# GpSimd sums four blocks of exponentials for one ones product, and row buffers are used in place

## Chip, cores and metric

One core of one Trainium2 chip runs the whole program. The metric is the device time in microseconds of one execution (median of three runs). TensorE (PE), VectorE (DVE), ScalarE (ACT), GpSimd (POOL) and SyncE (SP, which only issues DMAs here) each work through a fixed list of instructions in order; semaphores connect them.

## What is computed

A transformer block on x of shape 4 x 1024 x 512: layer norm, attention with 16 heads of 32, a projection, layer norm and a residual, then a gated feed-forward part (512 to 2048 to 512, weights stored as integers), again with norm and residual. The part that the change touches:

```python
scores = jnp.einsum('bsnh,btnh->bnst', k, q) / math.sqrt(HEAD_SIZE)
ones = jnp.ones_like(scores)
scores = jnp.triu(scores) + -10000.0 * jnp.tril(ones, k=-1)
attn = jax.nn.softmax(scores, axis=2)
out = jnp.einsum('bnkq,bnkh->bqnh', attn, v)
out = out.reshape(b, s, NUM_HEADS * HEAD_SIZE)
return out @ Wo + bo
```

The softmax runs over the first of the two sequence axes, and a column q sees the rows up to q.

## The kernel before

**Groups and steps.** Attention is done in 16 groups n (4 batches b, 4 groups of 4 heads, g = n mod 4). A group has 10 steps (STEPS): steps 0 to 2 take the first 512 queries (j = 0), steps 3 to 9 the second 512 (j = 1, kb = 0 to 6). A step takes one block kb of 128 keys (the last step of each j takes two short ones). The blocks kb = 0 to 3 of j = 1, steps 3 to 6, are wholly unmasked.

**One step on each engine.** TensorE makes the scores of four heads (score, L747); ScalarE writes their exponentials to Pt (L881), which has two buffers, so that step s + 2 overwrites those of step s. For the diagonal blocks (kb >= 4j) GpSimd then zeroes the masked part (L1180, two heads to an instruction). A step later TensorE multiplies the exponentials by a block of ones into PSUM bank DEN ("den", the softmax sums) and by V into bank NUM ("num"), both at L767, 8 matrix instructions of 512 columns each. Into the same loop are woven the maxima of the next group's scores ("mjob": PE L723 and L731, DVE L1006), the projections "qk", "vproj" and "woproj" (12 matmuls each at L710), at most one a step, and the layer-norm work of rows.

**Order.** order_of_jobs() writes one list PLAN; every engine walks it and takes its share, so each queue has the order of the list. A step emits: mjob, den and num of the step before, the four scores, invert and normalise where a j has ended, turns, the other row jobs, and at its end the projection that projections() names. row_work() assigns row jobs to steps by costs. Where a job is a "qk", GpSimd has a subtraction (L1173); a "dev" job is three small GpSimd instructions (L1134, L1137, L1145) that follow statistics of VectorE and precede a ScalarE normalisation (L811).

**Rows.** For each 128 rows t after woproj: yt (L1048), statistics, dev, wo_z into x1 (ACT), residual x1 + xr (DVE L1059), statistics, dev, norm2 (ACT), turn2 (PE transposes, ACT and DVE write x2s, DMA to x2d). yt, xr, x1 and x2s have two buffers each, by t mod 2. SP issues, in the list's order, among others 24 DMAs per group for "packs", the load of xr for t + 2 and the store of x1 at "residual", and the store of x2s at "turn2".

**PSUM.** Scores and maxima share five banks in turn, so that an mjob's second to fourth head wait until ScalarE has read the scores of the first to third head.

After attention the feed-forward part runs (gate_up at L781, down at L798), with the last row jobs in its first slots.

## Time and profile before

| | |
|---|---|
| median of three runs | 1789.68 us (1789.48 to 1794.05) |
| the profiled execution | 1788.66 us |
| its span | 1786.9 us |
| PE busy | 1636.9 us (92%) |
| DVE busy | 952.0 us (53%) |
| ACT busy | 744.8 us (42%) |
| POOL busy | 372.0 us (21%) |
| mean granted TensorE clock | 0.97 |

Attention runs from about 129 to 1090 us of the span, the feed-forward part from there to the end. Group 3 is the stretch 308.1 to 363.5 us, group 4 363.5 to 427.8, group 6 493.5 to 556.2, group 7 556.2 to 611.6, group 8 611.6 to 677.6, group 14 984.5 to 1039.2, group 15 1039.2 to 1090.5. Busy times are sums over instructions, with overlaps on one engine counted once; matmul ends are modelled, so that a run of them lasts about 0.2 us less than the row's figure suggests when the next one follows. A row of the timeline merges neighbouring instructions of one kind.

### The profile page before, as it was taken

The numbers are of one execution on the slowest core, as the hardware profiler recorded it, in microseconds if no ns is written. First come the engines' busy times: TensorE is split into PE (matmuls) and PEld (weight loads), VectorE is DVE, ScalarE is ACT, GpSimd is POOL, SyncE is SP. The second block draws the span as 40 slices with busy tenths as digits, with TensorE's granted clock in tenths as the row PEclk, the third lists the DMA queues.
The fourth block names the chain that finished last, engine by engine and source line by source line (L and its number), as shares of the span: only waits on it lengthen the run. The fifth ranks groups of instructions, "written<-read, shape, count | busy, mean of one in ns | idle before, by whom it ended". The sixth has DMA issues, their size and how long they took to land.

```text
span 1786.9 us, 25458 instructions
## 1 busy us (share of the span) xinstructions
PE 1636.9 (92%) x10015; PEld 691.6 (39%) x10016; DVE 952.0 (53%) x1785; ACT 744.8 (42%) x1207; POOL 372.0 (21%) x718
## 2 busy tenths in 40 slices
PE   2579999999989989999999879999999999999997
PEld 1223433333334433333333224444444444444443
DVE  3575656566666566755676623355334343435254
ACT  4314645556555556555465444323222222222221
POOL 2201422234233234222332232011000000000000
PEclk9889999999999999999999989999999999999999
DMA  6100121123122112201231453112010111110000
GB/s 220 45 21 16 48 61 33 28 77 102 31 71 55 49 56 82 71 22 47 54 93 43 136 186 136 42 56 92 30 41 36 36 36 36 42 53 28 21 24 24
DMA packets 59463, 106.28 MB, mean 59 GB/s; under 512 B 11472, under 2 KB 11472, under 8 KB 59088
## 3 DMA queue, kind: packets, MB, share of 16 engines
q1 hardware_dynamic: 59344, 104.66, 19.1%
q8 instruction: 79, 1.29, 0.3%
q14 instruction: 40, 0.33, 0.1%
HBM read 54.02 MB, written 25.17 MB: 44 GB/s over the span
## 4 chain that ended last, share of the span: by engine, by line
PE 75%; DVE 10%; ACT 9%; POOL 3%; issue 2%; DMA 1%; ACTq 0%; DVEq 0%; POOLq 0%
PE ps L781 24%; PE ps L710 17%; PE ps L767 13%; PE ps L798 12%; ACT pt L881 6%; PE ps L747 5%; DVE mcol L1006 4%; PE ps L723 2%; PE ps L731 2%; PE ps L677 1%; DVE st L908 1%; POOL rs L1137 1%; DMA xin<-in_x 1%; DVE v L996 1%; POOL rs L1145 0%
## 5 line engine op out<-in xcount | busy, mean ns | idle before, releaser
L881 ACT ACTIVATE pt<-ps,nrm 128x512 f32<-128x512 f32 (+1 forms) x640 | 360.7, 645 | 318.4 <-PE ps L747 317.9
L781 PE MATMUL ps<-x2in,gu 128*128 128x512 f16 x2048 | 464.3, 380 | 1.5 <-DVE yt L1048 1.5
L1006 DVE TENSOR_REDUCE mcol<-ps 128x1 f32<-128x512 f32 (+3 forms) x768 | 370.4, 548 | 117.3 <-PE ps L731 76.6
L781 PEld LDWEIGHTS ps<-x2in,gu 128*128 128x128 f16 x2048 | 200.7, 98 | 242.8 <-issue 2.4
L1081 DVE SCALAR_TENSOR_TENSOR hf<-ps,usc,sg 128x512 f32<-128x512 f32 x128 | 96.1, 751 | 265.3 <-PE ps L781 261.3
L798 PE MATMUL ps<-wd,hh 128*128 128x512 f16 x512 | 194.0, 379 | 0.0
L798 PE MATMUL ps<-wd,hl 128*128 128x512 f16 x512 | 194.0, 379 | 0.0
L897 ACT ACTIVATE hh<-hf 128x512 f16<-128x512 f32 x128 | 80.7, 630 | 256.5 <-DVE hf L1081 242.9
L767 PE MATMUL ps<-pt,ones 128*32 128x512 f32 (+3 forms) x1536 | 170.0, 508 | 18.1 <-POOL pt L1180 17.4
L747 PE MATMUL ps<-qpack,kpack 98*128 98x512 f16 (+3 forms) x768 | 165.4, 335 | 19.6 <-DVE mcol L1006 18.1
L1180 POOL TENSOR_SCALAR_AFFINE_SELECT pt<-pt 128x256 f32<-128x256 f32 (+1 forms) x192 | 95.7, 498 | 418.9 <-ACT pt L881 417.7
L892 ACT ACTIVATE sg<-ps,gsc 128x512 f32<-128x512 f32 x128 | 87.7, 685 | 220.7 <-PE ps L781 220.6
L1134 POOL TENSOR_SCALAR rs<-mv 128x1 f32<-128x1 f32 x128 | 24.6, 192 | 688.8 <-DVE mv L912 682.5
L767 PE MATMUL ps<-pt,v 128*32 128x512 f32 (+3 forms) x1536 | 165.9, 504 | 0.0
L1084 DVE TENSOR_TENSOR hl<-hf,hh 128x512 f16<-128x512 f32 x128 | 88.6, 692 | 96.6 <-ACT hh L897 96.6
L723 PE MATMUL ps<-stage 32*128 32x512 f16 (+3 forms) x768 | 102.1, 334 | 31.9 <-ACT pt L881 18.3
L747 PEld LDWEIGHTS ps<-qpack,kpack 98*128 98x128 f16 x768 | 59.4, 99 | 177.1 <-issue 113.5
L1173 POOL TENSOR_TENSOR stage<-tq,stage 128x512 f16<-128x512 f32 x64 | 74.4, 1163 | 158.4 <-ACT tq L871 158.4
L767 PEld LDWEIGHTS ps<-pt,v 128*32 128x32 f32 x1536 | 54.1, 112 | 75.5 <-issue 64.8
L677 PE MATMUL ps<-ident,xn 128*128 128x128 f32 x256 | 45.1, 305 | 36.1 <-ACT xn L811 27.4
L710 PE MATMUL ps<-xTh,wh 128*128 128x512 f16 x256 | 71.9, 406 | 6.7 <-ACT tq L871 6.7
L723 PEld LDWEIGHTS ps<-stage 32*128 32x128 f16 x768 | 27.3, 91 | 126.6 <-issue 51.2
(109 smaller groups left out, 1585.7 us busy)
## 6 DMA issues: line engine op xcount, KB each, us to landing
qpack<-stage SPq DMA_DIRECT2D x192, 64.0 KB, 2.0
kpack<-stage SPq DMA_DIRECT2D x192, 64.0 KB, 2.0
xin<-in_x SPq DMA_DIRECT2D x32, 256.0 KB, 2.7
xr<-in_x SPq DMA_DIRECT2D x32, 256.0 KB, 3.1
x1d<-x SPq DMA_DIRECT2D x32, 256.0 KB, 3.3
x2d<-x2s SPq DMA_DIRECT2D x32, 256.0 KB, 2.0
x2in<-x2d SPq DMA_DIRECT2D x8, 1024.0 KB, 5.6
x1in<-x1d SPq DMA_DIRECT2D x8, 1024.0 KB, 5.4
```

The source lines that it names most:

```text
L710: mm = pe.matmul(bk, lhsT, rhs, start=i == 0, stop=i == 11)
L723: mm = pe.matmul(bk[:, at:at + w], stage[rows, 0, 0, qb * 128:(qb + 1) * 128], stage[rows, 1, 0, k0:k0 + w], start=part == 0 or not diag, ...
L747: mm = pe.matmul(bk[:, at:at + 512 - q0], kp[0:98, h, kb_ * 128:(kb_ + 1) * 128], qp[0:98, h, j * 512 + q0:(j + 1) * 512], start=True, sto ...
L767: mm = pe.matmul((DEN if kind == "den" else NUM)[rows, q0:512], heads, Pt[:, ks, h, at:at + 512 - q0], start=kb_ == 0, stop=kb_ == 4 * j + 3)
L781: mm = pe.matmul(bk, GU[:, c, m, i * 128:(i + 1) * 128], x2in[:, 1 - k, :, p, c, :], start=p == 0 and c == 0, stop=p == 1 and c == 3)
L798: mm = pe.matmul(ps[:, 4 + s, :], src[:, n % 4, s * 128:(s + 1) * 128], WD[:, i, :], start=i == 0 and p == 0, stop=i == 15 and p == 1)
L881: act.activation(Pt[:, (step - 1) % 2, h, off:512], ps[:, BANK[job], off:512], ACT.Exp, scale=esc).then_inc(s_ex, 1)
L892: act.activation(sg[:, n % 2, :], ps[:, BANK["gate", n], :], ACT.Silu, scale=gsc[:, i:i + 1]).then_inc(s_sg, 1)
L1006: mm = dve.tensor_reduce(mcol[:, n % 2, col:col + 1], ps[:, BANK["max", n, i, h], at:at + w], AX.X, ALU.max)
L1081: dve.scalar_tensor_tensor(out=hf[:, n % 2, :], in0=ps[:, BANK["up", n], :], scalar=usc[:, i:i + 1], in1=sg[:, n % 2, :], op0=ALU.mult, op ...
L1084: dve.tensor_tensor(hl[:, n % 4, :], hf[:, n % 2, :], hh[:, n % 4, :], ALU.subtract).then_inc(s_hl, 1)
L1180: pool.affine_select(out=of, in_=of, compare_op=ALU.is_ge, fill=0.0, base=0, pattern=[[0, 2], [0, len(blocks(j, kb))], [1, 128]], channel_ ...
```

## The change

For the blocks kb = 0 to 3 of the second queries the ones products are left out. The exponentials of kb = 0 go to a third buffer of Pt (number 2); GpSimd adds those of kb = 1, 2 and 3 to it in place, one instruction for two heads (128 x 1024 float32), so two instructions for each of three blocks ("sum"). One ones product of the result, "den" n, 1, 0, is emitted in step 9. The exponentials that reuse a buffer now wait for the sum that reads it too (L881's wait). The sum of step s's block is emitted in step s + 1, after num.

In the list, dev jobs now stand at the head of their step, before mjob. For b > 0 and g = 0 the "qk" projections stand in steps 0, 2, 3, 7 in place of 1, 3, 7, 9 and woproj in 1, 5, 8, 9 in place of 0, 2, 5, 8. For room, the quotient is written into rec (atf goes), z into yt and the residual into xr (x1 goes), and x2s has one buffer; grow moves over Pt. The load of xr for t + 2 moves from residual t to turn2 t and waits for the store of xr t to land; turn2 waits for the store of x2s t - 1; woproj's yt waits for residual t - 2. In the feed-forward part the last woproj jobs stand in every second slot.

```diff
-        for i, s in enumerate(((1, 3, 7, 9), (0, 1, 2, 3), (1, 3, 7, 9), (1, 3, 5, 8))[g]):
+        for i, s in enumerate(((0, 2, 3, 7) if b else (1, 3, 7, 9), (0, 1, 2, 3), (1, 3, 7, 9), (1, 3, 5, 8))[g]):
             out[s] = ("qk", n + 2, i % 2, i // 2)
...
-        for i, s in enumerate(((0, 2, 5, 8), (5, 8))[g]):
+        for i, s in enumerate(((1, 5, 8, 9), (5, 8))[g]):
...
-            if kind == "wo_z" and ("wo_z", t - 2) in at and at.get(("norm2", t - 2), step) >= step:
+            if kind == "residual" and ("wo_stats", t - 2) in at and at.get(("turn2", t - 2), step) >= step:
...
+            here = rows.get(NS * n + s, [])
+            plan += [("dev", DEV_FOR[job[0]], job[1]) for job in here if job[0] in DEV_FOR]
             lot, of = (s + EARLY, n + 1) if s < NS - EARLY else (s + EARLY - NS, n + 2)
             if of < NG:
                 add(("mjob", of, lot))
             if pend is not None:
-                plan += [("den",) + pend, ("num",) + pend]
+                summed = pend[1] == 1 and pend[2] < 4
+                if not summed:
+                    add(("den",) + pend)
+                add(("num",) + pend)
+                if summed and pend[2] > 0:
+                    add(("sum",) + pend)
+                if s == NS - 1:
+                    add(("den", n, 1, 0))
             plan += [("score", n, j, kb, h) for h in range(4)]
             if pend is not None and last(*pend[1:]):
                 plan += [("invert",) + pend[:2], ("normalise",) + pend[:2]]
             if s == NS - EARLY and n + 1 < NG:
                 plan += [("mjoin", n + 1), ("mturn", n + 1)]
-            here = rows.get(NS * n + s, [])
             plan += [job for job in here if job[0] in ("ln1_turn", "turn2")]
-            for job in here:
-                if job[0] not in ("ln1_turn", "turn2"):
-                    plan += with_dev(job)
+            plan += [job for job in here if job[0] not in ("ln1_turn", "turn2")]
...
+    left = list(range(started, NT))
+    for i in range(2 * len(left) + len(LN2) - 1):
+        tail.append([each for k, t in enumerate(left) if 0 <= i - 2 * k <= len(LN2)
+                     for each in with_dev(((("woproj",) + LN2)[i - 2 * k], t))])
...
+SUMMED = [i for i, (j, kb) in enumerate(STEPS) if j == 1 and kb < 4]
+PBUF, BEFORE, used_by = {}, {}, {}
+for step in range(1, NS * NG + 1):
+    n, i = divmod(step - 1, NS)
+    buf = 2 if i == SUMMED[0] else (n * (NS - 1) + i - (i > SUMMED[0])) % 2
+    PBUF[step], BEFORE[step] = buf, used_by.get(buf)
+    used_by[buf] = step
+
...
-        Pt = A("pt", [128, 2, 4, 512], F32)
+        Pt = A("pt", [128, 3, 4, 512], F32)
+        grow = Map(A.at - 16384)("grow", [128, 2, 2048], F32)
...
+            def load_xr(t):
+                if t >= 2:
+                    e.wait_ge(d_o1[t % 2], 16 * (t // 2))
+                    e.wait_ge(s_xn, NORMED["turn2", t - 2])
+                sp.dma_start(xr[:, t % 2, :], xf[t * 128:(t + 1) * 128, :]).then_inc(d_xr[t % 2], 16)
+
...
-                        if t % 8 < 6:
-                            e.wait_ge(s_x1, NO[job])
-                            sp.dma_start(xr[:, t % 2, :], xf[(t + 2) * 128:(t + 3) * 128, :]).then_inc(d_xr[t % 2], 16)
                         e.wait_ge(s_x1, NO[job])
-                        sp.dma_start(x1d[t * 128:(t + 1) * 128, :], x1[:, t % 2, :]).then_inc(d_o1[t % 2], 16)
+                        sp.dma_start(x1d[t * 128:(t + 1) * 128, :], xr[:, t % 2, :]).then_inc(d_o1[t % 2], 16)
                     else:
-                        e.wait_ge(s_us, 2)
-                        if t >= 2:
-                            e.wait_ge(s_x1, NO["residual", t - 2])
-                        sp.dma_start(xr[:, t % 2, :], xf[t * 128:(t + 1) * 128, :]).then_inc(d_xr[t % 2], 16)
+                        load_xr(t)
                 elif kind == "turn2":
                     t = a[0]
+                    if t % 8 < 6:
+                        load_xr(t + 2)
                     e.wait_ge(s_x2h, NO[job])
                     e.wait_ge(s_x2l, NO[job])
-                    sp.dma_start(x2d[t], x2s[:, t % 2, :, :, :].rearrange("p a c n -> p (a c n)")
-                                 ).then_inc(d_o2[t % 2], 16)
+                    sp.dma_start(x2d[t], x2s[:].rearrange("p a c n -> p (a c n)")).then_inc(d_o2[t % 2], 16)
...
-                    ks = (STEP[a] - 1) % 2
+                    ks = PBUF[STEP[a]]
                     if kind == "den":
                         e.wait_ge(s_const, 7)
-                    if kb == 0 and (n, j) != (0, 0):
-                        e.wait_ge(s_dt if kind == "den" else s_at, 2 * n + j)
+                        if kb == 4 * j and (n, j) != (0, 0):
+                            e.wait_ge(s_dt, 2 * n + j)
+                        if kb < 4 * j:
+                            e.wait_ge(s_sum, 2 * NO["sum", n, 1, 3])
+                    elif kb == 0 and (n, j) != (0, 0):
+                        e.wait_ge(s_at, 2 * n + j)
...
-                                           Pt[:, ks, h, at:at + 512 - q0], start=kb_ == 0, stop=kb_ == 4 * j + 3)
+                                           Pt[:, ks, h, at:at + 512 - q0],
+                                           start=kb_ == (4 * j if kind == "den" else 0),
+                                           stop=kb_ == 4 * j + 3)
...
-                    if t >= 2:
-                        e.wait_ge(d_o2[t % 2], 16 * (t // 2))
-                    act.activation(x2s[:, t % 2, 0, :, :], ps[:, BANK[job], :].rearrange("p (c n) -> p c n", c=4),
+                    if t >= 1:
+                        e.wait_ge(d_o2[(t - 1) % 2], 16 * ((t - 1) // 2 + 1))
+                    act.activation(x2s[:, 0, :, :], ps[:, BANK[job], :].rearrange("p (c n) -> p c n", c=4),
...
-                    if step > 2:
-                        e.wait_ge(s_num, step - 2)
+                    if BEFORE[step] is not None:
+                        before = divmod(BEFORE[step] - 1, NS)
+                        e.wait_ge(s_num, BEFORE[step])
+                        if before[1] == SUMMED[0]:
+                            e.wait_ge(s_den, NO["den", before[0], 1, 0])
+                        elif before[1] in SUMMED:
+                            e.wait_ge(s_sum, 2 * NO[("sum", before[0]) + STEPS[before[1]]])
+                    if step > 1:
+                        e.wait_ge(s_us, 2)
                     e.wait_ge(s_sc, NO[job])
-                    act.activation(Pt[:, (step - 1) % 2, h, off:512], ps[:, BANK[job], off:512], ACT.Exp, scale=esc
+                    act.activation(Pt[:, PBUF[step], h, off:512], ps[:, BANK[job], off:512], ACT.Exp, scale=esc
...
-                    e.wait_ge(s_den, STEP[n, j, 4 * j + 2])
+                    e.wait_ge(s_den, NO["den", n, j, 4 * j + 2])
+                    if NO[job] > 1:
+                        e.wait_ge(s_al, NO[job] - 1)
...
-                        e.wait_ge(s_z, NO["wo_z", t - 2])
+                        e.wait_ge(s_x1, NO["residual", t - 2])
...
-                    dve.tensor_tensor(x1[:, k, :], x1[:, k, :], xr[:, k, :], ALU.add).then_inc(s_x1, 1)
+                    dve.tensor_tensor(xr[:, k, :], yt[:, k, :], xr[:, k, :], ALU.add).then_inc(s_x1, 1)
...
+                elif kind == "sum":
+                    n, j, kb = a
+                    e.wait_ge(s_num, STEP[n, 1, 0])
+                    for h in (0, 2):
+                        e.wait_ge(s_ex, NO["score", n, j, kb, h + 1])
+                        if kb > 1:
+                            e.wait_ge(s_sum, 2 * NO[job] - 3 + h // 2)
+                        pool.tensor_tensor(Pt[:, 2, h:h + 2, :], Pt[:, 2, h:h + 2, :], Pt[:, PBUF[STEP[a]], h:h + 2, :],
+                                           ALU.add).then_inc(s_sum, 1)
```

## Rows read from the trace of the kernel before

**Rows 1.** The page: busy shares, and the granted clock in 40 slices.
```profile
PE 1636.9 (92%) x10015; PEld 691.6 (39%) x10016; DVE 952.0 (53%) x1785; ACT 744.8 (42%) x1207; POOL 372.0 (21%) x718
PEclk9889999999999999999999989999999999999999
```

**Rows 2.** Stretch, its length, busy us of PE, PEld, DVE, ACT, POOL; PEclk; DMA.
```profile
308.10:363.50 55.40, 54.51 (x419) 21.72 (x417) 32.23 (x67) 29.09 (x50) 15.26 (x24) 1.00 0.15 39
363.50:427.80 64.30, 59.20 (x435) 24.07 (x434) 46.04 (x95) 37.07 (x62) 22.35 (x46) 0.97 0.27 79
...
493.50:556.20 62.70, 57.85 (x439) 23.55 (x439) 39.83 (x81) 34.21 (x58) 18.86 (x35) 1.00 0.21 60
...
984.50:1039.20 54.70, 42.35 (x299) 14.35 (x297) 29.03 (x56) 24.95 (x46) 15.66 (x26) 0.91 0.47 141
1039.20:1090.50 51.30, 41.89 (x276) 14.24 (x275) 14.81 (x24) 23.18 (x41) 19.45 (x27) 0.93 0.54 178
1090.50:1786.90 696.40, 681.87 (x3164) 310.29 (x3164) 293.00 (x467) 184.13 (x280) 42.82 (x111) 0.99 0.12 43
```

**Rows 3.** Timeline, group 7, steps 4 to 8: start, duration, instruction, idle before.
```profile
579.00 2.42 ACT L881 ACTIVATE pt<-ps,nrm 128x512 f32<-128x512 f32 x4 [1.11 <-PE ps L747]
...
587.20 1.06 PE L767 MATMUL ps<-pt,ones 128*32 128x512 f32 x8
...
588.08 1.04 PE L767 MATMUL ps<-pt,v 128*32 128x512 f32 x8
...
588.50 1.16 POOL L1173 TENSOR_TENSOR stage<-tq,stage 128x512 f16<-128x512 f32 x1 [9.01 <-ACT tq L871]
...
589.54 2.42 ACT L881 ACTIVATE pt<-ps,nrm 128x512 f32<-128x512 f32 x4 [1.12 <-PE ps L747]
...
594.43 2.42 ACT L881 ACTIVATE pt<-ps,nrm 128x512 f32<-128x512 f32 x4 [2.47 <-PE ps L747]
...
598.11 1.06 PE L767 MATMUL ps<-pt,ones 128*32 128x512 f32 x8
```

**Rows 4.** GpSimd's groups of instructions: busy, mean ns, idle before.
```profile
L1137 POOL TENSOR_TENSOR rs<-rs,half 128x1 f32<-128x1 f32 x128 | 72.1, 563 | 10.7 <-POOL rs L1134 0.2
L1180 POOL TENSOR_SCALAR_AFFINE_SELECT pt<-pt 128x256 f32<-128x256 f32 x128 | 54.5, 426 | 345.4 <-ACT pt L881 344.4 <-DVE atf L1039 0.7
...
L1192 POOL TENSOR_TENSOR atl<-atf,ath 128x512 f16<-128x512 f32 x32 | 37.1, 1161 | 2.7
L1145 POOL TENSOR_SCALAR rs<-rs,mv 128x1 f32<-128x1 f32 x96 | 27.9, 291 | 9.9
L1134 POOL TENSOR_SCALAR rs<-mv 128x1 f32<-128x1 f32 x128 | 24.6, 192 | 688.8 <-DVE mv L912 682.5
```

**Rows 5.** Timeline, group 6: exponentials of steps 4, 5; residual, dev; den of step 8.
```profile
522.65 1.26 ACT L881 ACTIVATE pt<-ps,nrm 128x512 f32<-128x512 f32 x2
...
527.78 2.42 ACT L881 ACTIVATE pt<-ps,nrm 128x512 f32<-128x512 f32 x4 [2.23 <-PE ps L747]
...
528.58 0.68 DVE L1059 TENSOR_TENSOR x<-x,xr 128x512 f32<-128x512 f32 x1
...
530.30 0.19 POOL L1134 TENSOR_SCALAR rs<-mv 128x1 f32<-128x1 f32 x1 [6.31 <-DVE mv L912]
...
542.71 1.06 PE L767 MATMUL ps<-pt,ones 128*32 128x512 f32 x8
```

**Rows 6.** Timeline around 892 us: two tensor-tensor operations on two engines.
```profile
891.89 1.15 POOL L1173 TENSOR_TENSOR stage<-tq,stage 128x512 f16<-128x512 f32 x1 [2.34 <-ACT tq L871]
...
892.21 1.38 DVE L1059 TENSOR_TENSOR x<-x,xr 128x512 f32<-128x512 f32 x1
```

**Rows 7.** Timeline of VectorE in group 8, step 3.
```profile
629.40 0.75 DVE L1048 SCALAR_TENSOR_TENSOR yt<-ps,nrm,bo_b 128x512 f32<-128x512 f32 x1 [6.09 <-ACT x L811]
```

**Rows 8.** TensorE's waits, 130 to 1090 us: total, times, longest.
```profile
PE ps L767 <- POOL pt L1180: 17.4, 11, 2.5
```

More of the change, by code:

```diff
@@ L220, in order_of_jobs @@
     started = max(job[1] for job in plan if job[0] == "woproj") + 1
-    for lot in staged(("woproj",) + LN2, list(range(started, NT))):
-        tail.append([each for job in lot for each in with_dev(job)])
+    left = list(range(started, NT))
+    for i in range(2 * len(left) + len(LN2) - 1):
+        tail.append([each for k, t in enumerate(left) if 0 <= i - 2 * k <= len(LN2)
+                     for each in with_dev(((("woproj",) + LN2)[i - 2 * k], t))])
     plan += [("load_x2", 1), ("load_x1", 0), ("load_x1", 1), ("load_ds",)]
@@ L387, in build @@
         atT = [A(f"at{p}", [128, 5, S], F16) for p in "hl"]
-        atf = A("atf", [128, 512], F32)
         rec = A("rec", [128, 512], F32)
@@ L393, in build @@
         xn = A("xn", [128, 2, 512], F32)
-        rows_at = A.at
         xr = A("xr", [128, 2, 512], F32)
         yt = A("yt", [128, 2, 512], F32)
-        x1 = A("x1", [128, 2, 512], F32)
-        x2s = A("x2s", [128, 2, 2, 4, 128], F16)
-        grow = Map(rows_at)("grow", [128, 2, 2048], F32)
-        assert A.at >= rows_at + 16384
+        x2s = A("x2s", [128, 2, 4, 128], F16)
         bo_b = A("bo_b", [128, 512], F32)
@@ L430, in build @@
         braw = R0("braw", [128, 1536], F32)
+        assert R0.at <= a2 + 40960
         R1 = Map(a1)
@@ L473, in build @@
             sem("s_" + name) for name in ("sc", "ex", "dg", "den", "num", "dt", "iv", "rc", "at", "ah", "al"))
+        s_sum = sem("s_sum")
         s_wo, s_yt, s_z, s_x1 = (sem("s_" + name) for name in ("wo", "yt", "z", "x1"))
@@ L832, in _ @@
                         e.wait_ge(s_tr, TURN_OF[no - 2])
-                    src, of_stats = (xin, "ln1_stats") if kind == "ln1_norm" else (x1, "residual")
+                    src, of_stats = (xin, "ln1_stats") if kind == "ln1_norm" else (xr, "residual")
                     normalised(xn[:, (no - 1) % 2, :], src[:, t % 2, :], (of_stats, t)).then_inc(s_xn, 1)
@@ L836, in _ @@
                     t = a[0]
-                    if t >= 2:
-                        e.wait_ge(s_xn, NORMED["turn2", t - 2])
-                        e.wait_ge(d_o1[t % 2], 16 * (t // 2))
-                    normalised(x1[:, t % 2, :], yt[:, t % 2, :], ("wo_stats", t)).then_inc(s_z, 1)
+                    normalised(yt[:, t % 2, :], yt[:, t % 2, :], ("wo_stats", t)).then_inc(s_z, 1)
                 elif kind == "ln1_turn":
@@ L930, in _ @@
                 elif kind == "turn2":
-                    k = a[0] % 2
                     e.wait_ge(s_x2h, NO[job])
-                    dve.tensor_tensor(x2s[:, k, 1, :, :], ps[:, BANK[job], :].rearrange("p (c n) -> p c n", c=4),
-                                      x2s[:, k, 0, :, :], ALU.subtract).then_inc(s_x2l, 1)
+                    dve.tensor_tensor(x2s[:, 1, :, :], ps[:, BANK[job], :].rearrange("p (c n) -> p c n", c=4),
+                                      x2s[:, 0, :, :], ALU.subtract).then_inc(s_x2l, 1)
                 elif kind == "bias_max":
@@ L1034, in _ @@
                     n, j = a
-                    if NO[job] > 1:
-                        e.wait_ge(s_al, NO[job] - 1)
                     e.wait_ge(s_rc, NO[job])
                     e.wait_ge(s_num, STEP[n, j, 4 * j + 2])
-                    dve.scalar_tensor_tensor(out=atf[:], in0=NUM, scalar=beta, in1=rec[:], op0=ALU.mult, op1=ALU.mult
+                    dve.scalar_tensor_tensor(out=rec[:], in0=NUM, scalar=beta, in1=rec[:], op0=ALU.mult, op1=ALU.mult
                                              ).then_inc(s_at, 1)
@@ L1058, in _ @@
                     e.wait_ge(s_z, NO["wo_z", t])
-                    dve.tensor_tensor(x1[:, k, :], x1[:, k, :], xr[:, k, :], ALU.add).then_inc(s_x1, 1)
+                    dve.tensor_tensor(xr[:, k, :], yt[:, k, :], xr[:, k, :], ALU.add).then_inc(s_x1, 1)
                     e.wait_ge(s_x1, NO[job])
-                    stats(x1[:, k, :], job)
+                    stats(xr[:, k, :], job)
                 elif kind == "ffn_load" and a[0] % 2 == 0:
@@ L1176, in _ @@
                     n, j, kb, h = a
-                    of = Pt[:, (STEP[a[:3]] - 1) % 2, h - 1:h + 1, begin(j, kb):blocks(j, kb)[0][1] + 128].rearrange(
+                    of = Pt[:, PBUF[STEP[a[:3]]], h - 1:h + 1, begin(j, kb):blocks(j, kb)[0][1] + 128].rearrange(
                         "p h (b n) -> p h b n", n=128)
@@ L1189, in _ @@
                     e.wait_ge(s_at, NO[job])
-                    pool.tensor_copy(atT[0][:, n % 5, cols], atf[:]).then_inc(s_ah, 1)
+                    pool.tensor_copy(atT[0][:, n % 5, cols], rec[:]).then_inc(s_ah, 1)
                     e.wait_ge(s_ah, NO[job])
-                    pool.tensor_tensor(atT[1][:, n % 5, cols], atf[:], atT[0][:, n % 5, cols], ALU.subtract).then_inc(s_al, 1)
+                    pool.tensor_tensor(atT[1][:, n % 5, cols], rec[:], atT[0][:, n % 5, cols], ALU.subtract).then_inc(s_al, 1)
                 elif kind == "ffn_load" and a[0] % 2 == 1:
```

1 line of the change is left out of this document (removed).

## Prediction

> **What bounds the kernel now.** I read the page first. TensorE is busy for 92% of the span [rows 1], no other engine above 53%, so what TensorE does and waits for sets the time. The busy time by stretch then says where this is strict. A plain attention group (g = 3) has 54.5 us of TensorE work in 55.4 us, and the feed-forward part 681.9 in 696.4 us [rows 2]: there a microsecond taken off TensorE is a microsecond of time, and a microsecond of waiting is one too. Groups with row work are looser: group 4 has 59.2 of 64.3 us and group 6 57.9 of 62.7 us; groups 14 and 15, which have no maxima to fill in, have 42 of 51 to 55 us [rows 2]. GpSimd looks idle: 15 to 22 us of each group. That is an average. What matters is where in its queue its work stands and who waits for it, so the third view is the timeline of a plain group [rows 3], with the mean durations of GpSimd's instructions beside it [rows 4].
>
> **What is removed.** A ones product of a full block goes from 587.20 to 588.08, where the product with V begins: 0.88 us [rows 3]. Four of them go in each group and one comes in step 9, so three net: 3 x 0.88 = 2.64 us a group, 16 x 2.64 = 42.2 us. In the plain groups all of it is on the path. In groups 14 and 15 a step is paced by the exponentials (2.42 us), but den still stands between the last exponential and the next scores, so I count it there too.
>
> **What is added on GpSimd.** Two additions of 128 x 1024 float32 for each of three blocks. The trace has no such instruction. The nearest row is the subtraction of 128 x 512 at 1.16 us (L1192) [rows 4]. Doubled it is 2.32 us; if some 0.19 us of it is fixed, as the one-column instruction L1134 suggests [rows 4], it is 0.19 + 2 x 0.97 = 2.13 us. I take 2.27 us and 0.08 us to the next, so 4.7 us for a block, with 4.4 and 4.8 as ends. The sum over 16 groups is 16 x 3 x 4.7 = 226 us of GpSimd's time. It has room for that in the mean, but the three blocks come one behind the other in steps 4 to 7, where a step becomes as short as 3.9 to 5 us.
>
> The Trainium skill, GPSIMD Engine Reference, section 4.1 (Engine selection), speaks against the choice: it would give an elementwise addition to VectorE, as GpSimd is about two times slower with two inputs. Its section 3.1 has 4497 ns for an addition of 2048 elements; half of that is 2.25 us, and the sum would be the same by it.
>
> **Who waits for the sums.** Three places. The exponentials of steps 6, 7 and 8 reuse the buffers that sums 1, 2 and 3 read. The den of step 9 needs all three; it is late enough. And the masking of step 7's block (L1180) stands behind the third sum in GpSimd's queue, while the den of step 8 on TensorE needs the masked block. Everything TensorE has stands behind that den. The wait is then: end of the third sum, plus two maskings (0.43 each and the gaps, 1.0 us), less the moment at which TensorE arrives.
>
> *Group 7 (and 3, 11), worked out.* Zero is the first exponential of step 4, 579.00 [rows 3]. TensorE comes to den of step 8 at 598.11, so at 19.1, and less 3 x 0.88 at 16.5. On GpSimd sum 1 can start when two heads are done, at 1.3, and ends at 6.0. But the qk of step 5 stands in the list before sum 2, and its subtraction waits for ScalarE: it starts at 588.50 = 9.5, now 8.6 (one den less ahead), and ends at 9.8 [rows 3]. GpSimd idles from 6.0 to 8.6. Sum 2 ends at 14.5, sum 3 at 19.2, the maskings at 20.2. TensorE waits 20.2 - 16.5 = 3.7 us. The exponentials of step 7 (at 594.43, now 12.8) wait for sum 2 until 14.5 as well, but TensorE has 2.6 us of projection to do meanwhile, so this is hidden. The group gains 2.64 and loses 3.7.
>
> *Groups 0 and 2.* Nothing stands between the sums (their qk comes in step 7): 1.3 + 3 x 4.7 = 15.4, masked at 16.4. TensorE arrives at about 16.5 as in group 7: no wait.
>
> *Group 6 (and 10).* A dev stands before sum 2, behind the residual of step 5. Zero is 522.65, step 5 begins at 5.1 (now 4.25), the residual's addition 0.8 us later, and the dev 1.7 us after the addition's start [rows 5]. The addition will meet sum 1 (below) and end at about 6.7; statistics and dev (0.19 + 0.56 + 0.29 and gaps, 1.2 us [rows 4]) end at about 8.9. Sum 2 ends at 13.6, sum 3 at 18.3, maskings at 19.3. TensorE arrives at 542.71 - 522.65 - 2.64 = 17.4 [rows 5]. It waits 1.9 us.
>
> *The rest is estimated from these.* Groups 4, 5, 8, 9 and 12 have the same dev before sum 2 and one more before sum 3 (1.2 us), with a slightly longer step 7: 2.4 us each. Groups 13 to 15 also have shorter steps (group 15 has integer conversions of weights between its sums): 3.3 us each. Group 1: 0.5 us. Sum: 3 x 3.7 + 2 x 1.9 + 5 x 2.4 + 3 x 3.3 + 0.5 = 37.3 us. With 4.4 us a block it is about 8 us less, and part of it replaces waits that stand there now (17.4 us of TensorE's waits are for this masking already [rows 8]). I take 33 us, with 15 and 45 as ends.
>
> **The row buffers in place.** In group 8, VectorE stood 6.1 us before yt, as it waited for wo_z two tiles back on ScalarE [rows 7]; TensorE ran out of banks behind it. Groups 4 and 12 have the same order. The new order puts the residual before, on VectorE's own queue, and spreads woproj, so this block goes: 1 to 3 us in each of three groups, I take 4 us in all. Against it stand new waits: woproj's yt waits for the residual before the last, turn2 for one store instead of the second last. On SP the load of xr is moved from residual to turn2, behind the landing of x1's store, and past the 24 packs DMAs where these come between; a residual comes at least two steps (10 us) after its turn2 in the list, more than a load needs. I cost these at nothing; if that cover is missing, VectorE stands for up to 3 us in a group with rows, and TensorE behind it. The moved dev jobs help ScalarE and are costed only as blocks in GpSimd's queue above. The wider spacing in the feed-forward part is nothing or a gain of up to 2 us. grow, rec and the start: nothing, all before or off the path.
>
> **The clock.** The granted clock is 1.2 instead of 2.4 GHz in some stretches: after TensorE's long waits at the start, in slice 27, and in groups 14 and 15, where it idles for a fifth of the time (0.91 and 0.93) [rows 1, 2]. Group 4, with 5 us idle, has 0.97, group 6 with as much idle has 1.00. A fall costs about 0.03 x 64 = 2 us. The new wait takes the plain groups from 1 to some 5 us idle, group 4's shrinks. I take one or two falls more: 3 us.
>
> **Sum.** 1788.7 (profiled execution) - 42.2 + 33 - 4 + 3 = 1778.5. The median is 1.0 above the profiled execution, so 1779.
>
> **Rivals.**
> *GpSimd keeps up.* If an addition takes 2.1 us or less and the rows' work fits in, waits fall to about 12 us: 1779 - 21 = 1758. For it: GpSimd is at 21% [rows 1], and sums without anything between end just in time. Against it: in group 7 the wait is made of list order, and shorter additions take only 1 us from it.
> *VectorE is held up.* At 892.21 an addition of two SBUF tiles on VectorE took 1.38 us, not 0.68, and ended 0.55 us after GpSimd's subtraction of 891.89 had ended (893.04) [rows 6]: it stood until that was over. GpSimd will now run such an instruction of 2.3 us nearly without pause for three steps of each group. Some ten residual additions and, where sums run late, the joining of maxima in step 8 fall in these steps. At 1 us for each of some 10 if VectorE's work behind it reaches TensorE: 1789, no change. The Trainium skill, GPSIMD Engine Reference, section 8 (Key points), names this: the two share their SBUF interfaces, with contention for VectorE instructions with two SBUF inputs. The trace agrees by the 1.38 us.
> *Slower: the clock falls after each new wait.* TensorE stands for 2 to 4 us in step 8 of thirteen groups. If each brings one more fall like group 4's at 2 us, this costs 26 us in place of 3: 1802. It decides from about five or six falls beyond my two, as 1779 + 5.5 x 2 passes 1790. For it: groups 14 and 15 with long waits in each step show many; against it: group 6.
>
> **Chances.** Forecast 0.44 (own range 1769 to 1790), GpSimd keeps up 0.19, VectorE held up 0.12, clock 0.25. A measurement of this kernel tells about 0.3% (5.4 us) from no change: 1784.3 to 1795.0. The forecast gives 0.29 faster, 0.14 same, 0.01 slower; the first rival 0.19 faster; the second 0.02, 0.06, 0.04; the third 0 faster, 0.04 same, 0.21 slower. Together 0.50, 0.24, 0.26. The range leaves out about 0.1 at each side: 1757 to 1800.
>
> **What would show it.** Right: half of the full-width ones products at L767 gone (three of six blocks a group); L1180 named as TensorE's releaser for some 30 us more, once per group at step 8, least in groups 0 and 2, most in 3, 7 and 11; groups 3, 7 and 11 no shorter than 55.4 us, groups 0 and 2 shorter by 2.6 us; additions of 2.1 to 2.4 us; the 6 us wait of rows 7 gone. Wrong: additions over 2.5 us; TensorE waiting for maxima instead (L1006 as releaser); VectorE waiting for xr's DMA; group 7 shorter.

## The result, and the profile after

| | before | after |
|---|---|---|
| median | 1789.58 us (1789.41 to 1794.05) | 1762.71 us (1762.46 to 1765.19) |
| ratio after / before | | 0.9847 (0.9829 to 0.9865) |
| the profiled execution's span | 1786.9 us | 1761.1 us |
| mean granted TensorE clock | 0.97 | 0.966 |

The change gains 27 us. The forecast was 1779, a gain of 10. The measured time lies outside the forecast's own range of 1769 to 1790 and inside the whole one of 1757 to 1800. The page of after, first its busy shares and the granted clock in 40 slices, then its row for the additions and for the ones products (to be read with [rows 1, 4]):

```profile
PE 1595.6 (91%) x9631; PEld 673.7 (38%) x9632; DVE 955.1 (54%) x1785; ACT 744.4 (42%) x1207; POOL 594.4 (34%) x814
PEclk9889999999999999999998779999999999999998
...
L1217 POOL TENSOR_TENSOR pt<-pt 128x1024 f32<-128x1024 f32 x96 | 225.1, 2373 | 5.0 <-ACT pt L909 4.5
...
L789 PE MATMUL ps<-pt,ones 128*32 128x512 f32 (+3 forms) x1152 | 113.6, 488 | 39.0 <-POOL pt L1207 31.9
```

TensorE has lost 384 matmuls and 41.3 us of busy time, GpSimd has 222 us more, and slices 22 to 24 have a lower clock. The same columns by stretch as in [rows 2], here for groups 3, 4, 6, 7, 14 and 15 and the feed-forward part:

```profile
304.80:363.70 58.90, 54.63 (x395) 21.16 (x393) 32.09 (x67) 29.02 (x50) 29.03 (x30) 0.94 0.14 36
363.70:420.80 57.10, 53.53 (x407) 21.76 (x405) 42.88 (x89) 34.53 (x59) 36.21 (x50) 1.00 0.26 76
482.60:541.50 58.90, 55.41 (x415) 22.71 (x416) 40.16 (x82) 34.39 (x59) 31.74 (x39) 1.00 0.21 58
541.50:599.30 57.80, 53.53 (x395) 20.94 (x393) 32.03 (x66) 28.99 (x49) 29.04 (x30) 0.97 0.15 37
952.50:1007.60 55.10, 44.23 (x274) 13.79 (x273) 30.09 (x56) 25.29 (x44) 29.70 (x29) 0.78 0.50 155
1007.60:1068.80 61.20, 46.55 (x261) 15.57 (x260) 17.59 (x26) 23.41 (x42) 34.60 (x33) 0.80 0.40 130
1068.80:1761.10 692.30, 677.87 (x3156) 309.00 (x3153) 290.94 (x463) 183.99 (x280) 42.52 (x111) 0.99 0.12 44
```

The plain groups 3 and 7 are longer than before (55.4), as forecast. Group 15 is 7.8 us longer, 61.1 us after 53.3, both counted to the end of the last quotient (the stretch above ends 2.1 us later in the work than that of [rows 2]). But group 4 is 7 us shorter with only 2.6 us of matmuls taken from it, and so are its like. So there is a gain in the groups with row work that the sum does not have, and the experiments had to find it.

The forecast wait in group 7, in the timeline of after (start, duration, instruction, idle before):

```profile
575.47 6.95 POOL L1217 TENSOR_TENSOR pt<-pt 128x1024 f32<-128x1024 f32 x3
...
577.89 2.42 ACT L909 ACTIVATE pt<-ps,nrm 128x512 f32<-128x512 f32 x4 [3.22 <-POOL pt L1217]
...
582.37 0.81 POOL L1207 TENSOR_SCALAR_AFFINE_SELECT pt<-pt 128x256 f32<-128x256 f32 x2
...
583.32 1.07 PE L789 MATMUL ps<-pt,ones 128*32 128x512 f32 x8 [2.87 <-POOL pt L1207]
...
584.17 1.89 PE L789 MATMUL ps<-pt,v 128*32 128x512 f32 x8
```

The last additions end at 582.42, two maskings follow, and TensorE has waited 2.87 us. Behind it the clock falls: eight products with V take 1.89 us where they took 1.04 [rows 3].

### The profile page after: what moved, and what is told of

Read it like the earlier page. It is cut to its first block, busy times and chain, and to the rows that moved or that the text cites. A ratio compares the mean times of both kernels' runs of the same rounds, so it can differ in the third digit from the quotient of the medians.

```text
span 1761.1 us, 24904 instructions
## 1 busy us (share of the span) xinstructions
PE 1595.6 (91%) x9631; PEld 673.7 (38%) x9632; DVE 955.1 (54%) x1785; ACT 744.4 (42%) x1207; POOL 594.4 (34%) x814
## 3 DMA queue, kind: packets, MB, share of 16 engines
q1 hardware_dynamic: 59344, 104.66, 19.4%
## 4 chain that ended last, share of the span: by engine, by line
PE 69%; DVE 11%; POOL 7%; ACT 6%; issue 4%; DMA 1%; ACTq 0%; DVEq 0%; POOLq 0%
PE ps L805 24%; PE ps L728 15%; PE ps L822 12%; PE ps L789 10%; DVE mcol L1033 5%; PE ps L765 4%; ACT pt L909 4%; POOL pt L1217 4%; PE ps L741 2%; DVE st L936 1%; PE ps L749 1%; PE ps L695 1%; DMA xin<-in_x 1%; POOL rs L1164 1%; POOL pt L1207 1%
## 5 line engine op out<-in xcount | busy, mean ns | idle before, releaser
L1217 POOL TENSOR_TENSOR pt<-pt 128x1024 f32<-128x1024 f32 x96 | 225.1, 2373 | 5.0 <-ACT pt L909 4.5
L765 PE MATMUL ps<-qpack,kpack 98*128 98x512 f16 (+3 forms) x768 | 180.8, 343 | 26.3 <-DVE mcol L1033 24.5
L1207 POOL TENSOR_SCALAR_AFFINE_SELECT pt<-pt 128x256 f32<-128x256 f32 (+1 forms) x192 | 94.7, 499 | 255.3 <-ACT pt L909 255.0
L789 PE MATMUL ps<-pt,v 128*32 128x512 f32 (+3 forms) x1536 | 174.0, 523 | 0.4 <-ACT pt L909 0.4
L789 PE MATMUL ps<-pt,ones 128*32 128x512 f32 (+3 forms) x1152 | 113.6, 488 | 39.0 <-POOL pt L1207 31.9
L741 PE MATMUL ps<-stage 32*128 32x512 f16 (+3 forms) x768 | 86.3, 336 | 22.4 <-DVE mcol L1033 14.1
L888 ACT ACTIVATE stage<-ps,abcol,nrm 128x512 f16<-128x512 f32 x64 | 49.8, 778 | 68.3 <-PE ps L728 68.0
L1164 POOL TENSOR_TENSOR rs<-rs,half 128x1 f32<-128x1 f32 x128 | 72.7, 568 | 10.7 <-POOL rs L1161 0.2
```

The source lines that it names most:

```text
L741: mm = pe.matmul(bk[:, at:at + w], stage[rows, 0, 0, qb * 128:(qb + 1) * 128], stage[rows, 1, 0, k0:k0 + w], start=part == 0 or not diag, ...
L765: mm = pe.matmul(bk[:, at:at + 512 - q0], kp[0:98, h, kb_ * 128:(kb_ + 1) * 128], qp[0:98, h, j * 512 + q0:(j + 1) * 512], start=True, sto ...
L789: mm = pe.matmul((DEN if kind == "den" else NUM)[rows, q0:512], heads, Pt[:, ks, h, at:at + 512 - q0], start=kb_ == (4 * j if kind == "den ...
L1164: pool.tensor_tensor(rs[:, m, 1:2], rs[:, m, 0:1], half[:, 0:1], ALU.pow).then_inc(s_rs, 1)
L1207: pool.affine_select(out=of, in_=of, compare_op=ALU.is_ge, fill=0.0, base=0, pattern=[[0, 2], [0, len(blocks(j, kb))], [1, 128]], channel_ ...
L1217: pool.tensor_tensor(Pt[:, 2, h:h + 2, :], Pt[:, 2, h:h + 2, :], Pt[:, PBUF[STEP[a]], h:h + 2, :], ALU.add).then_inc(s_sum, 1)
```

## Experiments

Every kernel was timed in three rounds beside the kernel before on the same chip; ratios are to that. A ratio of 0.01 is 17.9 us. The kernels fall into two families: parts of the order put into the kernel before, and the changed kernel with its additions altered.

**The order alone.** b1_new_slots is the kernel before with the new slots of the projections.

```diff
-        for i, s in enumerate(((1, 3, 7, 9), (0, 1, 2, 3), (1, 3, 7, 9), (1, 3, 5, 8))[g]):
+        for i, s in enumerate(((0, 2, 3, 7) if b else (1, 3, 7, 9), (0, 1, 2, 3), (1, 3, 7, 9), (1, 3, 5, 8))[g]):
...
-        for i, s in enumerate(((0, 2, 5, 8), (5, 8))[g]):
+        for i, s in enumerate(((1, 5, 8, 9), (5, 8))[g]):
```

> The kernel before, with only the projection slots of groups 4, 8 and 12 moved (qk to steps 0, 2, 3, 7, woproj to 1, 5, 8, 9). Nothing is summed on GpSimd, all buffers stay as they were. Theory A (the changed order of row work and projections gave most of the gain: groups 4, 8 and 12 fell from 64.3, 66.0, 64.7 us to 57.1): these groups fall by 5 to 7 us each, the time by 15 to 22 us, to 1768 to 1775. Theory B (the ones products saved gave the gain, GpSimd hides more than I had worked out): no more than 4 us, 1786 to 1790.

Measured: 1794.85 us, ratio 1.0046 (1.0029 to 1.0063). This is slower, outside both theories. Groups 4, 8 and 12 do fall, by 1.5, 4.2 and 3.3 us, but groups 5 and 9 grow from 65.7 to 70.9 and 68.7 us. The theory that the slots make the gain fell.

b2_dev_first is the kernel before with the dev jobs at the head of their step.

```diff
+            here = rows.get(NS * n + s, [])
+            plan += [("dev", DEV_FOR[job[0]], job[1]) for job in here if job[0] in DEV_FOR]
...
-            here = rows.get(NS * n + s, [])
...
-            for job in here:
-                if job[0] not in ("ln1_turn", "turn2"):
-                    plan += with_dev(job)
+            plan += [job for job in here if job[0] not in ("ln1_turn", "turn2")]
```

> The kernel before, with only the dev jobs moved to the head of their step. Theory A': the normalisations on ScalarE waited for dev jobs that stood late in GpSimd's queue, so this part alone gives 3 to 8 us, 1782 to 1787. Rival: GpSimd is idle ahead of most dev jobs and waits for VectorE's statistics, which do not come earlier; within 2 us of before, 1788 to 1791.

Measured: 1757.68 us, ratio 0.9839 (0.9824 to 0.9854): 29 us less, from the place of three tiny instructions in a list, and as much as the whole change brings (0.9847; the intervals overlap). Theory A' had the cause but only 3 to 8 us for it. The cause can be read where it acts. In the kernel before, group 6, step 0:

```profile
491.92 0.18 DVE L912 BATCH_NORM_AGGREGATE mv<-st 128x2 f32<-128x6 f32 x1
...
494.85 0.42 POOL L1180 TENSOR_SCALAR_AFFINE_SELECT pt<-pt 128x256 f32<-128x256 f32 x1 [3.52 <-ACT pt L881]
...
498.46 1.16 POOL L1192 TENSOR_TENSOR atl<-atf,ath 128x512 f16<-128x512 f32 x1
...
499.71 0.19 POOL L1134 TENSOR_SCALAR rs<-mv 128x1 f32<-128x1 f32 x1
...
500.94 0.81 ACT L811 ACTIVATE xn<-x,rs 128x512 f32<-128x512 f32 x1 [5.00 <-POOL rs L1145]
```

The statistics are there at 492.10. The dev is in GpSimd's queue behind the maskings and the split of the attention output (L1192), which themselves wait for other engines, and starts 7.6 us later. ScalarE stands 5.00 us before its normalisation with everything behind it, the exponentials of the next step too. The same place with the dev at the head of the step:

```profile
485.41 0.18 DVE L911 BATCH_NORM_AGGREGATE mv<-st 128x2 f32<-128x6 f32 x1
...
485.68 0.19 POOL L1133 TENSOR_SCALAR rs<-mv 128x1 f32<-128x1 f32 x1 [2.14 <-DVE mv L911]
...
486.99 2.42 ACT L880 ACTIVATE pt<-ps,nrm 128x512 f32<-128x512 f32 x4 [2.97 <-PE ps L746]
...
488.33 0.42 POOL L1179 TENSOR_SCALAR_AFFINE_SELECT pt<-pt 128x256 f32<-128x256 f32 x1 [1.46 <-ACT pt L880]
...
489.29 0.83 ACT L810 ACTIVATE xn<-x,rs 128x512 f32<-128x512 f32 x1
```

Now it starts 0.1 us after the statistics, and ScalarE has no idle time before the normalisation.

Part of the 29 us is TensorE's clock, which is higher where the waits are shorter. The stretch of group 4 is in before 64.30 us with 59.20 us of TensorE work at a granted clock of 0.97 [rows 2]; in b2 it is

```profile
365.60:425.40 59.80, 57.24 (x435) 23.54 (x434) 45.69 (x95) 36.73 (x62) 23.04 (x47) 1.00 0.30 85
```

So 2.5 us of the 4.5 are idle time that went, and 2.0 us are work of the same kind done faster. Over the whole span TensorE's busy time falls from 1636.9 to 1625.5 us with the same list of matmuls.

b4_dev_3to6 has the same edit for steps 3 to 6 only, to see whether the gain lies in the steps that the sums later fill.

```diff
+            here = rows.get(NS * n + s, [])
+            early = 3 <= s <= 6
+            if early:
+                plan += [("dev", DEV_FOR[job[0]], job[1]) for job in here if job[0] in DEV_FOR]
...
-                    plan += with_dev(job)
+                    plan += [job] if early else with_dev(job)
```

> The kernel before, with the dev jobs at the head of their step in steps 3 to 6 alone. Moving them in all steps gave -28.8 us (b2). In steps 3 to 6 GpSimd has no masking, and a dev job at either place is the same for its queue, but for the normalise of step 3. Theory Q (the gain is the place in GpSimd's queue: a dev job behind this step's maskings cannot start until ScalarE has made the exponentials, and ScalarE then stands before the normalisation): almost nothing, within 4 us of before. Rival R (any earlier dev job helps, in all steps alike): two fifths of it or more, -9 to -15 us.

Measured: 1778.52 us, ratio 0.9949 (0.9934 to 0.9964): 9 us of the 29, at the lower end of rival R and more than theory Q allows. In groups 6 and 10 step 3 falls from 8.44 to 6.53 us; there the split of the attention output stands ahead of the dev. The longest steps of before stay: from the first exponential of step 3 to that of step 4 groups 4, 8 and 12 have 11.12, 11.12 and 11.47 us, here still 10.92 to 11.79, and only in b2 6.8 to 6.9. With step 0 of groups 5, 6, 9 and 10 (7 us together from b4 to b2) this is about the 20 us that b4 leaves. They come with the devs of steps 7 to 2, where the maskings stand ahead, in step 0 the split too; that half was not run by itself.

How long ScalarE stood before all its normalisations until GpSimd's dev was done (us, times), in before, b1, b4, b2 and after:

```profile
  POOL rs L1145: 144.3, 67
```
```profile
  POOL rs L1145: 146.5, 70
```
```profile
  POOL rs L1149: 126.7, 61
```
```profile
  POOL rs L1144: 33.6, 13
```
```profile
  POOL rs L1172: 40.2, 14
```

Inside attention alone (130 to 1090 us in before, to the end of attention in the others) it is 111.9 us in 56 places in before, 91.0 in 50 in b4, 0.3 in 2 in b2, and nothing in after. What is left in the last two rows lies ahead of attention and in the feed-forward part.

x5_dev_old is the changed kernel with the dev jobs put back.

```diff
-            plan += [("dev", DEV_FOR[job[0]], job[1]) for job in here if job[0] in DEV_FOR]
...
-            plan += [job for job in here if job[0] not in ("ln1_turn", "turn2")]
+            for job in here:
+                if job[0] not in ("ln1_turn", "turn2"):
+                    plan += with_dev(job)
```

> The changed kernel with the dev jobs back at their old place in the step, behind the maskings, the normalise, and now the sums too. The head-of-step place gave -28.8 us alone (b2). If the result of the changed kernel rests on that move, this is 29 to 45 us slower than it: 1792 to 1808, slower than before. If the new slots and buffers give the gain as well without it, 1763 to 1775.

Measured: 1801.96 us, ratio 1.0061 (1.0042 to 1.008), and the wait above is 159.9 us in 76 places. Without the dev move the change is slower than before, as a dev can then also stand behind the sums.

**The additions.** x1_no_sums is the changed kernel, order and buffers included, with no block summed and all ones products back.

```diff
+def sums(n):
+    return False
...
-                summed = pend[1] == 1 and pend[2] < 4
+                summed = pend[1] == 1 and pend[2] < 4 and sums(n)
...
-                                           start=kb_ == (4 * j if kind == "den" else 0),
+                                           start=kb_ == (4 * j if kind == "den" and sums(n) else 0),
...
```

> The changed kernel without its sums: each of the four blocks gets its ones product again, GpSimd adds nothing; order, buffers and waits stay new. Theory A: order and buffers are worth some 20 us and the sums only 5 to 9, so 1767 to 1772. Theory B: the sums are worth 20 us or more, so 1783 or above. Groups 3, 7 and 11 return from 57.9 to 55.4 us by either.

Measured: 1751.16 us, ratio 0.9799 (0.9784 to 0.9813), faster than either theory had it. The interval does not touch that of the changed kernel: the sums that give the change its name cost 0.0048 of the time, 8.6 us; the gain of 36 us is all in order and buffers.

x8_tiny_adds keeps every instruction and wait of the changed kernel, but each addition covers 32 of the 512 columns, so that the softmax sums of the second queries are incomplete.

```diff
-                        pool.tensor_tensor(Pt[:, 2, h:h + 2, :], Pt[:, 2, h:h + 2, :], Pt[:, PBUF[STEP[a]], h:h + 2, :],
+                        pool.tensor_tensor(Pt[:, 2, h:h + 2, 0:32], Pt[:, 2, h:h + 2, 0:32], Pt[:, PBUF[STEP[a]], h:h + 2, 0:32],
```

> The changed kernel with all sums in place, waits and ones products as they are, but each addition over 32 of 512 columns only (the softmax sums of the second queries are then incomplete). It measures what the three ones products less would be worth if GpSimd's time for them were near nothing. By the count of 42.2 us from x1_no_sums (ratio 0.980, 1751 us): 1709 to 1714 us, and no wait for the masking in step 8. If the steps without den are held by something else (VectorE's maxima, the exponentials), then 1720 to 1735.

Measured: 1732.89 us, ratio 0.9697 (0.9681 to 0.9713). The additions take 0.32 us each. Against x1 this is what the missing ones products are worth when adding is nearly free: 0.0102, 18 us, not 42. Against the changed kernel it is what the additions' length costs: 0.0150, 27 us.

Where the ones products' time goes is in TensorE's waits (130 to 1060 us of the span; total, times, longest), first x1, then x8, then the changed kernel:

```profile
PE ps L794 <- POOL pt L1212: 18.7, 15, 2.4
...
PE ps L769 <- DVE mcol L1038: 10.1, 25, 4.9
```
```profile
PE ps L765 <- DVE mcol L1033: 25.7, 85, 4.9
PE ps L789 <- POOL pt L1207: 18.9, 15, 2.5
```
```profile
PE ps L789 <- POOL pt L1207: 31.9, 20, 3.6
PE ps L765 <- DVE mcol L1033: 24.5, 82, 4.9
```

From x1 to x8 TensorE's busy time falls from 1622.8 to 1580.5 us, the 42.3 us that the forecast took off, but 20 us of it come back as idle time. Its waits for the maxima (mcol, whose banks the scores take over) grow by 15.6 us in 60 more places: it arrives earlier and VectorE does not. From x8 to the changed kernel the waits for the masked blocks (L1207) grow by 13 us, and two new ones of 7.0 us together, in groups 14 and 15, are put down to "issue".

The lengths of the groups (first exponential of one group to that of the next, group 15 to the end of the last quotient, from the timelines, us) show which groups give the time back:

```
group            0    1    2    3    4    5    6    7    8    9   10   11   12   13   14   15
before        62.7 60.0 56.8 55.4 64.3 65.7 62.7 55.4 66.0 65.7 64.2 55.4 64.7 56.8 54.7 53.3
b2 dev first  63.1 58.8 56.8 55.4 59.8 61.6 59.6 55.4 59.8 61.6 59.6 55.4 59.8 55.2 52.7 55.2
x1 no sums    63.1 58.9 56.9 55.4 56.9 63.4 59.6 55.4 56.9 63.4 59.6 55.4 56.9 57.7 52.8 54.2
x8 tiny adds  60.7 55.0 55.4 53.1 56.0 61.5 58.8 53.1 56.0 63.2 58.8 53.1 56.0 57.3 55.1 50.5
after         60.7 57.7 55.4 58.9 57.1 61.8 58.8 57.9 57.1 61.8 58.8 57.8 57.1 60.5 55.1 61.1
y1 3 blocks   61.3 58.5 56.0 53.8 56.1 62.5 58.9 53.8 56.1 61.7 58.9 53.8 56.1 54.8 53.3 52.2
```

From x1 to x8 groups 0 to 3, 7 and 11 give 14.7 us of 6 x 2.64 = 15.8. The other ten give 8.2 of 26.4. The stretch of group 6 in x1 and x8, columns as before, shows it: TensorE's busy time falls by 2.2 us, the length by 0.7.

```profile
486.80:546.40 59.60, 57.60 (x439) 23.62 (x439) 39.85 (x81) 34.38 (x59) 17.89 (x32) 1.00 0.20 56
```
```profile
474.70:533.60 58.90, 55.41 (x415) 22.71 (x416) 40.16 (x82) 34.39 (x59) 19.85 (x39) 1.00 0.21 58
```

The expectations below took group 15 of x1 as 53.1 us, and so 8.0 us as what the sums cost there; to the same point of the work it is 54.2 us, and they cost 6.9.

**Where sums pay.** s1_sums_in_seven sums only in groups 0, 1, 2, 5, 6, 9 and 10, those in which the changed kernel was no longer than x1; x2_sums_to_12 leaves out groups 13 to 15. Both are x1 with another condition:

```diff
 def sums(n):
-    return False
+    return n in (0, 1, 2, 5, 6, 9, 10)
```

> The changed kernel, with sums only in groups 0, 1, 2, 5, 6, 9 and 10; the other nine groups take the ones products again. By the group lengths of the changed kernel against x1_no_sums (-2.4, -1.2, -1.5, -1.6, -0.8, -1.6, -0.8) this is x1 less 10 us: 1741, with 1738 to 1745. If a group's length depends on its neighbours' sums, or the clock falls elsewhere, it lies nearer to x1: 1746 to 1753.

Measured: 1745.04 us, ratio 0.9762 (0.9743 to 0.9781), 6.6 us under x1 by ratio where 10 were expected.

> The changed kernel without sums in the last three groups, 13 to 15. By the group lengths these three lose 2.8, 2.3 and 8.0 us by their sums: 13 us less than the changed kernel, about 1750. Rival: the stalls there are not from the sums but from the weights' loads and conversions in the same queue, and remain; then within 4 us of the changed kernel.

Measured: 1750.0 us, ratio 0.9791 (0.9776 to 0.9805), as forecast. The three groups cost 10 us of the changed kernel's time, and what is left of the sums in groups 0 to 12 is about nothing against x1 (intervals overlap).

x3_qk_at_7 takes the subtraction from between the sums in the groups g = 3: their third qk goes from step 5 to 7, and a woproj from 7 to 5.

```diff
-        for i, s in enumerate(((0, 2, 3, 7) if b else (1, 3, 7, 9), (0, 1, 2, 3), (1, 3, 7, 9), (1, 3, 5, 8))[g]):
+        for i, s in enumerate(((0, 2, 3, 7) if b else (1, 3, 7, 9), (0, 1, 2, 3), (1, 3, 7, 9), (1, 3, 7, 8))[g]):
...
-        for i, s in enumerate((5, 7, 9) if n == NG - 1 else (7, 9)):
+        for i, s in enumerate((5, 7, 9) if n == NG - 1 else (5, 9)):
```

> The changed kernel, with the third qk of groups 3, 7 and 11 moved from step 5 to step 7 and the woproj of step 7 to step 5, so that no subtraction stands between the sums. If the wait of these groups in step 8 comes from the qk ahead of sum 2 in GpSimd's queue, it goes, and the groups fall from 57.9 to about 53 us: 1763 - 3 x 5 = 1748, with 1746 to 1753. Rival: the additions themselves are too slow for the short steps (2.36 us each), then TensorE still waits for 2 us or more there and the time is 1757 to 1763.

Measured: 1759.57 us, ratio 0.9846 (0.9831 to 0.9861), the same as the changed kernel. The time missed its forecast of 1746 to 1753. Groups 3, 7 and 11 did what was expected: they fall from 58.9, 57.9 and 57.8 to 54.2 us, and TensorE's wait in them from 2.9 to 1.0 us each, so most of it is made of the list's order, as worked out. But groups 4, 8 and 12 go from 57.1 to 58.7 and groups 5 and 9 from 61.8 to 63.4, as the row work moves with the projection, and the clock is low in groups 13 to 15 in both.

y1_three_blocks sums only kb = 0, 1 and 2 (two additions a pair of heads, two ones products fewer); y2_three_to_13 the same without groups 14 and 15. Against x1, beside the condition on n (true, and n < 14):

```diff
-                summed = pend[1] == 1 and pend[2] < 4 and sums(n)
+                summed = pend[1] == 1 and pend[2] < 3 and sums(n)
...
-                        first = 4 * j if sums(n) else 0
+                        first = 3 * j if sums(n) else 0
...
```

> The changed kernel, but only the blocks kb = 0 to 2 are summed: two blocks of additions in place of three, the block kb = 3 has its own ones product, and two ones products net are saved. Theory S (TensorE's new wait is the third sum, which ends after TensorE has come to step 8): the chain of sums ends 4.9 us earlier and the wait goes in all groups but perhaps the last ones, so nearly two thirds of the 18 us that tiny additions gave remain: 1751 (x1) - 12 = 1739, with 1736 to 1744. Rival (any sum work disturbs, through VectorE and the exponentials' buffers, in proportion): halfway between x1 and the changed kernel, 1751 to 1759.

Measured: 1735.95 us, ratio 0.9700 (0.9681 to 0.9718), as Theory S had it.

> As the one before, and no sums in groups 14 and 15, where conversions of weights share GpSimd's queue. If these two still lose by their sums as with three blocks (2.3 and 8.0 us), it is 4 to 8 us faster than with sums in all groups; if two blocks fit there as well, it is 2 to 4 us slower.

Measured: 1734.92 us, ratio 0.9686 (0.9671 to 0.9701). Not to be told from y1, so neither forecast holds: two blocks fit in groups 14 and 15 as well, but bring little there. Both beat the kernel before and after; this one is 0.0161 under the changed kernel, 29 us. TensorE's waits in y2:

```profile
PE ps L769 <- DVE mcol L1038: 21.5, 80, 4.9
PE ps L794 <- POOL pt L1212: 17.5, 15, 2.4
```

The second row stands where it stood with no sums at all (18.7): these waits are in groups 2, 6, 10 and 13 to 15, in x1 as in y2. With the third block's additions gone the sums make no masking late, and two ones products fewer bring as much (0.0099 against x1) as three do with free additions (0.0102).

## Why the prediction was right in sign and wrong in size and reason

In ratios of 1788 us: order and buffers 36 us less (x1), ones products 18 us less (x8 against x1), the additions' length 27 us more (after against x8); together 27 less. The forecast had 4 less, 42 less, and 33 and 3 more; together 10 less. The right sign is luck: the prediction had the sums gain 6 us and order and buffers 4, and the sums lost 9 us while order and buffers gained 36 us.

**The step that failed: "The moved dev jobs help ScalarE and are costed only as blocks in GpSimd's queue".** It costs the move at nothing on the side where it helps. It brings 29 us alone (b2) and 38 us in the changed kernel (x5 against after, 0.0214). The evidence stood in the trace of before: ScalarE, busy for 42%, idle for 144.3 us in front of 67 of its normalisations, 111.9 us of it inside attention, because of instructions of 0.2 to 0.6 us on an engine that is at 21% [rows 1, 4]. The prediction read TensorE's waits, and there no dev is named: within attention TensorE waits for banks that ScalarE's exponentials (18.3 us) or VectorE's maxima (18.1) have still to read, and for maskings (17.4). With the dev move alone the first two fall to 13.8 and 9.3 us. The step should have been: of every moved instruction, ask who waits for it now and how long, on each engine.

**The second: "three net: 3 x 0.88 = 2.64 us a group, 16 x 2.64 = 42.2 us".** It measured 18 us by ratio, 22 in the profiled executions. The work taken off TensorE is right (42.3 us), and nearly all of it comes back where there is no slack (2.3 us in each plain group, x1 to x8). Wrong is counting it in the ten groups that the prediction had itself called looser: [rows 2] has 59.2 of 64.3 us for group 4, and there the maxima, row work and exponentials pace the steps. The errors hid each other: 32 us too little here, 24 too much there, and the waits 9 too dear, so that 17 of the measured gain were missing.

**Waits for the masked block: the sum right, its parts not.** 33 and 3 for the clock were forecast, 27 measured by ratio. In the profiled executions after is 32 us longer than x8, and of these TensorE's idle time is 17 us and its busy time, for the same list of matmuls, 15 us (1580.5 to 1595.6) at a lower clock. So the waits were costed at about twice, the clock at a fifth of what they are.

The chain of group 7 came out as worked out: from the first exponential of step 4 the sums end at 6.1, 14.4 and 19.0 us and the maskings at 19.9 (forecast 6.0, 14.5, 19.2 and 20.2), TensorE comes at 17.0 (16.5) and waits 2.87 (3.7). In the other groups the error is when TensorE comes. In group 6 the sums end at 18.1 (forecast 18.3), but TensorE comes at 19.1, not 17.4, and there is no wait. In groups 4, 8 and 12 they end at 19.4 and TensorE comes at 19.2, for a wait of 1.1; in 5 and 9 they end at 21.2 and it comes at 22.1, for none. The ones products taken out bring it forward by only 1.0 us in groups 4 and 6 (20.1 in x1, 19.1 in x8), which is the second error again.

By group lengths, after against x8, the costs add up to 34.0 us beside the 37.3 worked out. Groups 3, 7 and 11: 11.1 forecast, 15.3 measured (in group 7 2.9 of wait and 1.9 of slower work). Groups 0 and 2: none and none. Groups 13 to 15: 9.9 and 13.8, 10.6 of it in group 15, with a clock of 0.80. Groups 4, 5, 8, 9 and 12: 12 and 2.2. Groups 6 and 10: 3.8 and 0. Group 1: 0.5 and 2.7. That the two sums lie so near is luck. The naming row grew by 14.5 us (17.4 in [rows 8], 31.9 after), not by 30. The 17.4 us lie in groups 13 to 15 alone and mostly in other steps, so they took little off the new waits.

**The additions: right.** 2.27 us assumed, 2.36 measured (median; 2.34 to 2.80). The Trainium skill, GPSIMD Engine Reference, section 4.1 (Engine selection), would not have put them on GpSimd but on VectorE. No run here gave them to VectorE, so that choice is not tested. What the runs show is that on GpSimd three additions a pair of heads cost more than the ones products they replace bring, and two pay (0.0099).

**Row buffers.** VectorE's 6 us before yt [rows 7] are gone, but the buffers are not needed for that: with the slots alone (b1) these three waits are gone too, and with the dev move alone (b2) they are 3.5 to 3.6 us. What the buffers bring by themselves was not measured. x1 against b2, for slots, buffers and the spacing in the feed-forward part together, is 0.0040, 7 us, where 4 were forecast. Groups 4, 8 and 12 gain 3 us each there, groups 5 and 9 lose 2 each and group 13 loses 2.5, and the feed-forward part is 2 us shorter (694.4 for 696.5).

**The rivals.** GpSimd keeps up (1758) comes nearest in time but for another reason: it does not keep up. VectorE held up: the residual additions have a median of 0.68 us and a longest of 1.03, the joining of maxima 0.33 instead of 0.17, and VectorE's whole busy time is 955.1 us after 950.7 in x8, so this took little. The clock: 26 us in place of 3 were its price, and the 15 us of slower work are more than half of that. A lower clock than in x8 is seen in groups 1, 3, 7, 11, 13, 14 and 15, seven and not thirteen. The reading of "slice 27" is off: the slice with a lower clock in before, after the start, is the 24th [rows 1], which lies in groups 14 and 15 themselves. No term hangs on it.

## What to carry to other kernels

Ask of every engine, not only of the one at 92%, what its idle time ends on: long waits for tiny instructions mean that these stand behind something slow in an in-order queue, and here moving them forward cost little (in b2 only groups 0 and 15 are longer, by 0.4 and 1.9 us). Work taken off the busiest engine is worth its full time only in stretches where that engine has no slack; multiply by those groups, not by all. When work is moved to an idle engine, find the largest amount that still ends before the next item in its queue is due: here the additions of two blocks, not of three.
